# Pairing two 8x8 areas of one head in the score operands of a windowed attention kernel

## The chip, the cores and the metric

One NeuronCore of a Trainium2 chip runs the whole program. The metric is the device time of one execution in microseconds (us).

## The reference

The input x is (2, 128, 128, 128): batch, channels, rows, columns. Two residual blocks follow each other:

```
x = x + attention(gn(x));  x = x + conv3x3(gn(x)) + bias      gn: 32 groups of 4 channels
attention(x): g = clip((x*ac_w + ac_b)*x, 0, 6)
  qkv = qkv_w @ g                       16 heads of 8 channels; areas ("windows") of 8x8 = 64 pixels
  per area and head: o = softmax(q k^T / sqrt(8)) v
  out = proj_w @ o + proj_b
```

## The kernel before

Channels lie on the 128 partitions and the image of one batch stays in SBUF. For each batch the attention runs over 32 **units** of 8 areas (UT = 512 pixels); then the convolution runs over 16 strips of 8 rows. Its two phases are untouched by the change except for the memory that they lend.

The attention is a software pipeline. Every engine has its own list of steps per iteration i, written out by hand in a function `one`; `live(k)` says that unit i+k exists, and the step with n+k works k units ahead. The engines meet only at semaphores (`after` waits for the count of a unit). For one unit the steps are:

1. DVE makes aff, gpre and g32 (L667, L679, L703), ACT the high f16 part of g (L472), POOL the low part (L380).
2. PE projects keys and queries into the PSUM banks GB and GA (`project`, L853 to L855, three matmuls of 512 columns each) and the values in `v_rows` (L872, 12 matmuls of 128 columns).
3. ACT copies the high f16 part of q and k out of PSUM (L503, L495), DVE subtracts for the low part (L690, L692).
4. SP writes both to DRAM and reads them back in another layout. `write` (L261, L262) sends, per unit and operand, parts lo and hi (256 KB) and once more the high part (128 KB); `queries_in` (L272) reads 4 x 96 KB, `keys_in` (L280) 2 x 192 KB. On the score operands' 64 rows per row half r lie 48 rows of channel parts (two heads j, 8 channels, 3 parts) and two rows for the row maxima. Queries of head j stand in columns j, zeros elsewhere: `q_bd` holds [r, g, j, pixel].
5. `scores` (L885) does, for each of 4 pairs p of areas, 32 matmuls of 48 rows, 64 weights' columns and 64 moving columns, on the four quarters of the array (row half r, column half w). They fill the two banks S_B, of which there is one pair. DVE takes the row maxima from them (`row_max`, L654). PE turns the maxima of a unit (L975), ACT and DVE split them (L499, L686), and `maxima` (L288, 4 transfers of 8 KB) puts them into q_bd.
6. `scores_t` (L899) computes the scores again, transposed and with the maxima subtracted: 8 matmuls per pair of areas with 128 rows, 64 weights' columns and 256 moving columns, on two column halves. ACT takes the exponential (L448).
7. `weigh` (L918, L926) multiplies with the values and the ones, ACT and DVE make the quotient, POOL refines it (L370, L372), PE projects (L995), ACT and POOL add to the image (L476, L385), DVE collects statistics (L698).

The score operands have BUFS = 3 buffers, so the reads for unit d wait for the last `scores_t` of unit d-3 (`after(sp, st_done, d - BUFS)`). SP runs one list:

```
if live(3): queries_in(n + 3); keys_in(n + 3)
if live(2): maxima(n + 2)
if live(4): write(0, n + 4); write(1, n + 4)
```

SP's iteration i runs while PE is in its iteration i+1. PE projects unit n+3 in its iteration n and needs what was read in for n+2 before `scores(n + 2, 0)`, the third last score step of an iteration.

## Time and profile before

| what | value |
|---|---|
| three runs | 1206.22, 1206.10, 1197.05 us (median 1206.1) |
| profiled execution, whole time | 1207.08 us |
| its span | 1205.3 us, mean granted TensorE clock 0.947 |
| PE busy | 1015.8 us (84%) |
| weight loads (PEld) busy | 582.6 us (48%) |
| DVE busy | 983.1 us (82%) |
| ACT busy | 791.3 us (66%) |
| POOL busy | 503.8 us (42%) |
| L899 / L885 matmuls, busy | 163.8 us (x2048) / 118.6 us (x8192) |
| DMA | 140.59 MB, q1 share of 16 engines 36.3% |

Busy times of one engine count each instant once. PE and PEld overlap; "issue" is time in which the engine waited for nothing that the profile shows. Between the first and last L975 of a batch lie 31 units: from 67.1 to 443.9 us and from 663.1 to 1030.4 us.

### The profile page before, as it was taken

What the parts mean: (1) busy time and instruction counts of PE and PEld (TensorE: products, weight loads), DVE (VectorE), ACT (ScalarE), POOL (GpSimd) and SP (SyncE); (2) the same over time, 40 slices, a digit from 0 to 9 for tenths busy, and PEclk for the clock granted to TensorE, in tenths of its full rate; (3) what the DMA queues carried; (4) which work ended last, traced back from release to release, by engine and by line L of the source; (5) the groups of instructions that cost most, each with busy time, mean ns of one, the idle gap of its engine ahead of it and who ended that gap; (6) DMA issues with size and microseconds to landing.
All of it is one profiled execution on the core that took longest, in us unless ns stands there. A gap on an engine that the chain in (4) does not pass through costs nothing.

```text
span 1205.3 us, 52690 instructions
## 1 busy us (share of the span) xinstructions
PE 1015.8 (84%) x23011; PEld 582.6 (48%) x23011; DVE 983.1 (82%) x1312; ACT 791.3 (66%) x1327; POOL 503.8 (42%) x469
## 2 busy tenths in 40 slices
PE   0388999999999985998853899999999999779996
PEld 0155565556555652433321555556655655334442
DVE  6786888889888754899986788888988976379996
ACT  1257787778778774655532688878887877556663
POOL 5214454445444433233343245545454544404335
PEclk9879999999999997999986899999999999879998
DMA  8234444444444420133343454444444444001112
GB/s 307 84 118 125 136 138 138 136 137 128 135 142 135 142 64 1 44 129 108 105 157 122 123 150 139 136 137 138 144 132 148 134 142 126 4 1 53 70 70 88
DMA packets 114917, 140.59 MB, mean 117 GB/s; under 512 B 25088, under 2 KB 91008, under 8 KB 113664
## 3 DMA queue, kind: packets, MB, share of 16 engines
q1 hardware_dynamic: 114688, 137.23, 36.3%
q8 instruction: 182, 2.98, 1.1%
q14 instruction: 47, 0.39, 0.1%
HBM read 67.96 MB, written 67.11 MB: 112 GB/s over the span
## 4 chain that ended last, share of the span: by engine, by line
PE 63%; DVE 18%; issue 8%; DMA 4%; ACT 3%; SPq 2%; POOL 2%; POOLq 0%; DVEq 0%; ACTq 0%
PE ps L918 11%; PE ps L899 11%; PE ps L926 9%; PE ps L885 8%; PE ps L995 6%; PE ps L853 5%; DVE work L760 5%; PE ps L854 5%; PE ps L855 5%; DVE work L756 4%; PE ps L872 4%; DVE st L610 1%; SPq L288 1%; DVE work L738 1%; DMA q_bd<-stack_scratch 1%
## 5 line engine op out<-in xcount | busy, mean ns | idle before, releaser
L654 DVE TENSOR_REDUCE m_all<-ps 128x16 f32<-128x1024 f32 x256 | 313.5, 1225 | 114.9 <-PE ps L885 114.3
L370 POOL TENSOR_SCALAR work<-work 128x256 f32<-128x256 f32 x128 | 108.6, 849 | 401.2 <-DVE work L647 352.4
L885 PEld LDWEIGHTS ps<-k_pl,q_bd 48*64 48x64 f16 x8192 | 90.4, 111 | 174.5 <-issue 126.9
L448 ACT ACTIVATE late_probs<-ps,ws 128x1024 f32<-128x1024 f32 x128 | 142.8, 1116 | 44.6 <-PE ps L899 42.8
L853 PE MATMUL ps<-work,c_hi 128*128 128x512 f16 x384 | 148.3, 386 | 27.7 <-DVE work L760 27.7
L899 PE MATMUL ps<-q_bd,k_pl 128*64 128x256 f16 x2048 | 163.8, 282 | 7.5 <-ACT work L448 4.0
L885 PE MATMUL ps<-k_pl,q_bd 48*64 48x64 f16 x8192 | 118.6, 198 | 57.3 <-issue 39.4
L536 ACT CAST work<-work 128x512 f16<-128x512 f32 (+1 forms) x128 | 79.0, 622 | 115.8 <-DVE work L756 107.9
L448 ACT ACTIVATE work<-ps,ws 128x1024 f32<-128x1024 f32 x128 | 141.7, 1107 | 13.1 <-PE ps L899 11.5
L854 PE MATMUL ps<-work,c_lo 128*128 128x512 f16 x384 | 148.0, 385 | 0.0
L855 PE MATMUL ps<-work,c_hi 128*128 128x512 f16 x384 | 147.4, 384 | 0.0
L380 POOL TENSOR_TENSOR g_both<-work,g_both 128x512 f16<-128x512 f32 x64 | 99.9, 1561 | 54.4 <-ACT g_both L472 54.4
L899 PEld LDWEIGHTS ps<-q_bd,k_pl 128*64 128x64 f16 x2048 | 93.2, 110 | 58.7 <-issue 24.7
L647 DVE TENSOR_TENSOR work<-ps,work 128x512 f32<-128x512 f32 x128 | 87.3, 682 | 26.1 <-ACT work L457 26.1
L400 POOL TENSOR_TENSOR work<-work,img 128x512 f32<-128x512 f32 x30 | 48.1, 1603 | 139.3 <-DVE work L756 124.6
L760 DVE TENSOR_TENSOR work<-work 128x512 f16<-128x512 f32 (+1 forms) x128 | 101.7, 810 | 3.7 <-ACT work L536 3.1
L489 ACT COPY v_ext<-ps 64x256 f32<-64x256 f32 x256 | 93.3, 364 | 13.0 <-PE ps L872 8.1
L372 POOL TENSOR_TENSOR work<-work 128x256 f32<-128x256 f32 x128 | 93.2, 728 | 10.7
L455 ACT ACTIVATE work<-ps 128x256 f32<-128x256 f32 x128 | 49.2, 384 | 68.5 <-PE ps L926 68.5
L756 DVE TENSOR_TENSOR work<-g_both 128x512 f32<-128x512 f32 (+1 forms) x128 | 86.1, 693 | 4.8 <-ACT g_both L527 2.6
L918 PE MATMUL ps<-late_probs,v_ext 128*32 128x64 f32 x4096 | 87.6, 226 | 1.8 <-issue 1.6
L995 PE MATMUL ps<-work,pw 128*128 128x512 f32 x128 | 78.5, 698 | 7.0 <-POOL work L372 7.0
(126 smaller groups left out, 1894.1 us busy)
## 6 DMA issues: line engine op xcount, KB each, us to landing
stack_scratch<-work SPq DMA_DIRECT2D x128, 256.0 KB, 2.4
q_bd<-stack_scratch SPq DMA_DIRECT2D x256, 96.0 KB
k_pl<-stack_scratch SPq DMA_DIRECT2D x128, 192.0 KB, 3.5
stack_scratch<-work SPq DMA_DIRECT2D x128, 128.0 KB, 2.5
out_dram<-work SPq DMA_DIRECT2D x32, 512.0 KB, 2.9
img<-in_x_dram SPq DMA_DIRECT2D x8, 1024.0 KB, 13.4
img<-in_x_dram SPq DMA_DIRECT2D x16, 512.0 KB, 4.3
q_bd<-m_pair SPq DMA_DIRECT2D x256, 8.0 KB
```

Source lines behind the costliest of these rows:

```text
L370: g.tensor_scalar(near[h], near[h], -2.0, None, ALU.add).then_inc(less_done, 1)
L448: a.activation(probs[h][:, p % 2, :], ps[:, ST_B:ST_B + 2, :].rearrange("p w t -> p (w t)"), ACT.Exp, scale=ws[:, R_EXP:R_EXP + 1]).then_i ...
L654: v.tensor_reduce(m_all[:, 0, :, p], ps[:, S_B:S_B + 2, :].rearrange("p r (a k) -> p (r a) k", k=WIN), AX.X, ALU.max).then_inc(max_done, 1)
L756: v.tensor_tensor(plane[i][:, new_rows(t), :], column(t, l), column(t, r), op).then_inc(planes_done, 1)
L760: v.tensor_tensor(x_lo[:, i, ring_rows(t), :], plane[i][:, new_rows(t), :], x_hi[:, i, ring_rows(t), :], ALU.subtract).then_inc(x_lo_done, 1)
L853: t_.matmul(o, lhs_hi, rhs_hi, start=first, stop=False)
L854: t_.matmul(o, lhs_lo, rhs_hi, start=False, stop=False)
L855: return t_.matmul(o, lhs_hi, rhs_lo, start=False, stop=last)
L885: mm = t_.matmul(ps[64 * w:64 * w + 64, S_B + r, at:at + WIN], q_bd[rows, md, r, g, j, tok], k_pl[rows, md, g, tok], start=True, stop=True)
L899: mm = t_.matmul(ps[64 * c:64 * c + 64, ST_B + w, a * 256:a * 256 + 256], k_pl[:, md, g, tok], q_bd[:, md, :, g, :, tok], start=True, stop ...
L918: mm = t_.matmul(ps[32 * k:32 * k + 32, PV_B + h, at:at + WIN], v_ext[:, md, EACH * p + w, k, j:j + 2, :].rearrange("p s y -> p (s y)"), p ...
L995: t_.matmul(ps[:, GB, :], pw[:, :], o_n, start=True, stop=True).then_inc(proj_done, 1)
```

## The change

The score operands get another layout, and the queue of preparations gets one unit longer.

- On the 48 rows of a row half now lie 8 channels of **one** head, times two areas e of a pair (HE = 2), times 3 parts; the 8 heads of a half lie along g (HG = 8). A query of area 0 has zeros on the rows of area 1 and the other way round. These zeros are in the buffer `q_flat`, set by POOL once at the start and once ahead of batch 1 (the convolution's output buffer c_out[1] lies there), and they are sent along: the queries' writes and reads double (512 + 256 KB written, 2 x 384 KB read per unit). Keys hold 64 columns per pair: as many bytes as before, in rows of 512 bytes in place of 1 KB when read.
- `scores`: per pair of areas 16 matmuls of 48 rows, 128 weights' columns and 64 moving columns, on two row halves, in place of 32 on quarters.
- `scores_t`: per pair of areas 16 matmuls of 64 rows, 64 weights' columns and 128 moving columns on four quarters, in place of 8 on column halves.
- Projections of q and k, their splitting and their writes come 4 units ahead, not 3 (FIRST = 6); g gets four buffers. `queries_in` and `keys_in` of a unit now come one SP iteration after its writes (except for the first three units), behind the next unit's writes.
- The order of heads in probs, v and the output becomes the natural one, and proj_w is loaded by one transfer. SP issues 12 transfers per unit, not 14.

```
-HR, HG, HJ = 2, 4, 2
+HR, HG, HJ, HE = 2, 8, 2, 2
...
-ROWS = HJ * HD * PARTS
-HROWS = HD * PARTS
...
-FIRST = 5
+FIRST = 6
+G_BUFS = 4
...
-W_AT = -4
+W_AT = -5
...
-    stackd = nc.dram_tensor("stack_scratch", [BUFS, 2, P, PARTS, UT], F16, kind="Internal").ap()
+    q_stack = nc.dram_tensor("q_stack", [BUFS, P, HE, PARTS, UT], F16, kind="Internal").ap()
+    k_stack = nc.dram_tensor("k_stack", [BUFS, P, HE, PARTS, UT // HE], F16, kind="Internal").ap()
...
-        k_pl = sb("k_pl", [P, BUFS, HG, UT], F16)
-
-        q_bd = sb("q_bd", [P, BUFS, HR, HG, HJ, UT], F16)
+        k_pl = sb("k_pl", [P, BUFS, HG, UT // HE], F16)
+
+        q_bd = sb("q_bd", [P, BUFS, HG, UT], F16)
...
-        qk = part(1536, 1024).bitcast(F16).rearrange("p (s t) -> p s t", s=4)
+        k_parts = part(1536, 512).bitcast(F16).rearrange("p (e s x) -> p e s x", e=HE, s=2)
+        q_flat = part(7936, 1344).bitcast(F16)
+        g_parts = [(g_both[:, s * UT:s * UT + UT] if s < BUFS else part(2048, UT)).bitcast(F16).rearrange("p (k t) -> p k t", k=2)
+                   for s in range(G_BUFS)]
...
+        q_parts = q_flat[:, 0:2 * HE * UT].rearrange("p (e s t) -> p e s t", e=HE, s=2)
+
+        def queries(s):
+
+            both = q_flat[:, s * UT:s * UT + HE * (2 * UT + WIN)].rearrange("p (e y) -> p e y", e=HE)[:, :, 0:UT]
+            return both.rearrange("p e (a f t) -> p a e f t", a=PAIRS, f=HE)[:, :, :, 0, :]
+
+        def keys(s):
+
+            return k_parts[:, :, s, :].rearrange("p e (a t) -> p a e t", a=PAIRS)
+
+        def by_window(bank):
+
+            return ps[:, bank, :].rearrange("p (a e t) -> p a e t", a=PAIRS, e=HE)
...
-                def write(which, d, md, lo, sent):
-                    after(sp, lo, d)
-                    to = stackd[md, which]
-                    sp.dma_start(to[:, 0:2, :], qk[:, 2 * which:2 * which + 2, :]).then_inc(sent, 16)
-                    sp.dma_start(to[:, 2, :], qk[:, 1 + which, :]).then_inc(sent, 16)
+                def write_queries(d, md):
+                    after(sp, q_lo_done, d)
+                    sp.dma_start(q_stack[md, :, :, 0:2, :].rearrange("p e s t -> p e (s t)"),
+                                 q_parts.rearrange("p e s t -> p e (s t)")).then_inc(q_sent, 16)
+                    sp.dma_start(q_stack[md, :, :, 2, :], q_parts[:, :, 1, :]).then_inc(q_sent, 16)
+
+                def write_keys(d, md):
+                    after(sp, k_lo_done, d)
+                    sp.dma_start(k_stack[md, :, :, 0:2, :].rearrange("p e s x -> p e (s x)"),
+                                 k_parts.rearrange("p e s x -> p e (s x)")).then_inc(k_sent, 16)
+                    sp.dma_start(k_stack[md, :, :, 2, :], k_parts[:, :, 0, :]).then_inc(k_sent, 16)
 
                 def queries_in(d, md):
                     after(sp, q_sent, d)
                     after(sp, st_done, d - BUFS)
                     after(sp, q_in, d - 1)
-                    q_rows = stackd[md, 0].rearrange("(r g j d) s t -> r j (d s) g t", r=HR, g=HG, j=HJ)
+                    q_rows = q_stack[md].rearrange("(r g d) e s t -> r (d e s) g t", r=HR, g=HG)
                     for r in range(HR):
-                        for j in range(HJ):
-                            at = 64 * r + HROWS * j
-                            sp.dma_start(q_bd[at:at + HROWS, md, r, :, j, :], q_rows[r, j]).then_inc(q_in, 16)
+                        sp.dma_start(q_bd[64 * r:64 * r + ROWS, md, :, :], q_rows[r]).then_inc(q_in, 16)
 
                 def keys_in(d, md):
                     after(sp, k_sent, d)
                     after(sp, st_done, d - BUFS)
                     after(sp, k_in, d - 1)
-                    k_rows = stackd[md, 1].rearrange("(r g a) s t -> r (a s) g t", r=HR, g=HG)
+                    k_rows = k_stack[md].rearrange("(r g d) e s x -> r (d e s) g x", r=HR, g=HG)
                     for r in range(HR):
                         sp.dma_start(k_pl[64 * r:64 * r + ROWS, md, :, :], k_rows[r]).then_inc(k_in, 16)
 
...
                     for r in range(HR):
                         for k in range(2):
                             at = 64 * r + ROWS + k
-                            sp.dma_start(q_bd[at:at + 1, md, r, :, :, :].rearrange("o g j (a t) -> o (g j a) t", a=PAIRS),
+                            sp.dma_start(q_bd[at:at + 1, md, :, :].rearrange("o g (a t) -> o (g a) t", a=PAIRS),
                                          m_pair[32 * r:32 * r + 32, k, :]).then_inc(m_in, 16)
 
                 def one(i, m, live):
                     n = i + b * UNITS
-                    if live(3):
-                        queries_in(n + 3, (m + 3) % BUFS)
-                        keys_in(n + 3, (m + 3) % BUFS)
                     if live(2):
                         maxima(n + 2, (m + 2) % BUFS)
-                    if live(4):
-                        after(sp, q_in, n + 1)
-                        write(0, n + 4, (m + 4) % BUFS, q_lo_done, q_sent)
-                        after(sp, k_in, n + 1)
-                        write(1, n + 4, (m + 4) % BUFS, k_lo_done, k_sent)
+                    if live(5):
+                        after(sp, q_in, n + 2)
+                        write_queries(n + 5, (m + 5) % BUFS)
+                        after(sp, k_in, n + 2)
+                        write_keys(n + 5, (m + 5) % BUFS)
+                    if live(5) and i + 5 < BUFS:
+                        queries_in(n + 5, (m + 5) % BUFS)
+                        keys_in(n + 5, (m + 5) % BUFS)
+                    if live(4) and i + 4 >= BUFS:
+                        queries_in(n + 4, (m + 4) % BUFS)
+                        keys_in(n + 4, (m + 4) % BUFS)
...
+                    after(pool, out_done, b * CUNITS - 3)
+                    g.memset(q_flat[:, 0:2 * HE * UT].bitcast(F32), 0.0).then_inc(q_zero, 1)
...
+                    if live(4):
+                        to = g_parts[(i + 4) % G_BUFS]
+                        after(pool, g_hi_done, n + 4)
+                        g.tensor_tensor(to[:, 1, :], g32, to[:, 0, :], ALU.subtract).then_inc(g_lo_done, 1)
...
+                    if live(5):
+                        if b and i + 5 == BUFS:
+                            after(act, conv_done, b * CUNITS - 1)
+                        after(act, g32_done, n + 5)
+                        after(act, v_done, n + 5 - G_BUFS)
+                        a.copy(g_parts[(i + 5) % G_BUFS][:, 0, :], g32).then_inc(g_hi_done, 1)
...
-                        after(act, k_done, n + 3)
-                        after(act, k_sent, n + 2)
-                        a.copy(qk[:, 2, :], ps[:, GB, :]).then_inc(k_hi_done, 1)
+                    if live(4):
+                        after(act, k_done, n + 4)
+                        after(act, k_sent, n + 3)
+                        a.copy(keys(0), by_window(GB)).then_inc(k_hi_done, 1)
...
-                    if live(3):
-                        after(act, q_done, n + 3)
-                        after(act, q_sent, n + 2)
-                        a.copy(qk[:, 1, :], ps[:, GA, :]).then_inc(q_hi_done, 1)
+                    if live(4):
+                        if i + 4 == 0:
+                            act.wait_ge(q_zero, b + 1)
+                        after(act, q_done, n + 4)
+                        after(act, q_sent, n + 3)
+                        a.copy(queries(1), by_window(GA)).then_inc(q_hi_done, 1)
...
-                    if live(3):
-                        after(dve, q_hi_done, n + 3)
-                        v.tensor_tensor(qk[:, 0, :], ps[:, GA, :], qk[:, 1, :], ALU.subtract).then_inc(q_lo_done, 1)
-                        after(dve, k_hi_done, n + 3)
-                        v.tensor_tensor(qk[:, 3, :], ps[:, GB, :], qk[:, 2, :], ALU.subtract).then_inc(k_lo_done, 1)
+                    if live(4):
+                        after(dve, q_hi_done, n + 4)
+                        v.tensor_tensor(queries(0), by_window(GA), queries(1), ALU.subtract).then_inc(q_lo_done, 1)
+                        after(dve, k_hi_done, n + 4)
+                        v.tensor_tensor(keys(1), by_window(GB), keys(0), ALU.subtract).then_inc(k_lo_done, 1)
...
                     after(pe, max_done, d, p)
                     for g in range(HG):
-                        for j in range(HJ):
-                            for w in range(EACH):
-                                tok = slice((EACH * p + w) * WIN, (EACH * p + w + 1) * WIN)
-                                at = g * P + j * WIN
-                                for r in range(HR):
-                                    rows = slice(64 * r, 64 * r + ROWS)
-                                    mm = t_.matmul(ps[64 * w:64 * w + 64, S_B + r, at:at + WIN],
-                                                   q_bd[rows, md, r, g, j, tok], k_pl[rows, md, g, tok],
-                                                   start=True, stop=True)
+                        for r in range(HR):
+                            rows = slice(64 * r, 64 * r + ROWS)
+                            mm = t_.matmul(ps[:, S_B + r, g * WIN:g * WIN + WIN],
+                                           q_bd[rows, md, g, p * P:p * P + P], k_pl[rows, md, g, p * WIN:p * WIN + WIN],
+                                           start=True, stop=True)
                     mm.then_inc(s_done, 1)
...
-                    for w in range(EACH):
-                        tok = slice((EACH * p + w) * WIN, (EACH * p + w + 1) * WIN)
-                        for g in range(HG):
-                            a, c = g // 2, g % 2
-                            mm = t_.matmul(ps[64 * c:64 * c + 64, ST_B + w, a * 256:a * 256 + 256],
-                                           k_pl[:, md, g, tok], q_bd[:, md, :, g, :, tok],
+                    for g in range(HG):
+                        k, c = g // 2, g % 2
+                        for r in range(HR):
+                            rows = slice(64 * r, 64 * r + 64)
+                            mm = t_.matmul(ps[64 * c:64 * c + 64, ST_B + r, k * P:k * P + P],
+                                           k_pl[rows, md, g, p * WIN:p * WIN + WIN], q_bd[rows, md, g, p * P:p * P + P],
                                            start=True, stop=True)
                     mm.then_inc(st_done, 1)
...
                         else:
-                            after(pe, k_lo_done, n + 2)
-                        after(pe, g_lo_done, n + 3)
-                        project(1, GB, (m + 3) % BUFS, k_done)
+                            after(pe, k_lo_done, n + 3)
+                        after(pe, g_lo_done, n + 4)
+                        project(1, GB, (i + 4) % G_BUFS, k_done)
```

## Rows read from the trace of the kernel before

**Rows 1.** Fourth part of the page: the chain that ended last, by engine.

```profile
PE 63%; DVE 18%; issue 8%; DMA 4%; ACT 3%; SPq 2%; POOL 2%; POOLq 0%; DVEq 0%; ACTq 0%
```

**Rows 2.** Windows: us; PE, PEld, DVE, ACT, POOL busy; clock; DMA share; GB/s.

```profile
79.10:443.90 364.80, 341.22 (x10206) 213.48 (x10204) 299.98 (x375) 284.49 (x501) 170.87 (x175) 0.98 0.44 132
675.90:1030.40 354.50, 335.60 (x10205) 211.16 (x10204) 300.92 (x374) 283.80 (x500) 170.84 (x175) 1.00 0.46 136
...
350.30:361.50 11.20, 11.20 (x343) 7.02 (x341) 10.54 (x14) 9.67 (x19) 6.03 (x7) 1.00 0.40 126
```

**Rows 3.** Timeline of PE in that one unit: start us, us.

```profile
350.35 0.27 PE L975 MATMUL ps<-ident,m_all 128*128 128x128 f32 x1
...
352.55 0.45 PE L885 MATMUL ps<-k_pl,q_bd 48*64 48x64 f16 x32
...
356.95 0.63 PE L899 MATMUL ps<-q_bd,k_pl 128*64 128x256 f16 x8
357.51 0.45 PE L885 MATMUL ps<-k_pl,q_bd 48*64 48x64 f16 x32
357.88 0.29 PE L872 MATMUL ps<-w_hi,g_both 128*128 128x128 f16 x2
...
358.56 0.38 PE L853 MATMUL ps<-g_both,w_hi 128*128 128x512 f16 x1
```

**Rows 4.** Timeline of the weight loads (PEld) in that unit.

```profile
360.82 0.10 PEld L853 LDWEIGHTS ps<-g_both,w_hi 128*128 128x128 f16 x1
360.83 0.10 PEld L854 LDWEIGHTS ps<-g_both,w_lo 128*128 128x128 f16 x1
```

**Rows 5.** Timeline of DVE in that unit; in brackets idle before and its releaser.

```profile
349.82 1.18 DVE L679 SCALAR_TENSOR_TENSOR work<-img,cf,work 128x512 f32<-128x512 f32 x1
...
353.06 1.23 DVE L654 TENSOR_REDUCE m_all<-ps 128x16 f32<-128x1024 f32 x1 [0.28 <-PE ps L885]
...
360.95 1.18 DVE L679 SCALAR_TENSOR_TENSOR work<-img,cf,work 128x512 f32<-128x512 f32 x1
```

**Rows 6.** Chain of waits from 285 to 305 us, in order of time.

```profile
292.90 3.67 DMA stack_scratch<-work
...
299.09 3.77 DMA q_bd<-stack_scratch
...
304.06 0.45 PE ps L885 x32
```

**Rows 7.** Waits of the whole run: engine, line, awaited: us, times, longest.

```profile
PE ps L885 <- issue: 39.4, 34, 4.6
```

**Rows 8.** Timeline of SP's queue around one unit's transfers, and the PE rows near it.

```profile
313.98 2.42 SPq L288 DMA_DIRECT2D q_bd<-m_pair  x4
316.49 0.54 SPq L261 DMA_DIRECT2D stack_scratch<-work  x1
...
319.54 2.50 SPq L272 DMA_DIRECT2D q_bd<-stack_scratch  x4
322.15 0.79 SPq L280 DMA_DIRECT2D k_pl<-stack_scratch  x2
...
315.19 0.45 PE L885 MATMUL ps<-k_pl,q_bd 48*64 48x64 f16 x32
```

**Rows 9.** Windows with the DMA share and rate in the last two columns.

```profile
12.00:24.00 12.00, 1.59 (x6) 1.10 (x6) 11.05 (x29) 1.93 (x3) 9.22 (x1) 1.00 1.01 427
316.50:317.40 0.90, 0.90 (x22) 0.41 (x11) 0.90 (x2) 0.85 (x1) 0.00 (x0) 1.00 0.12 30
341.50:342.50 1.00, 1.00 (x28) 0.83 (x18) 1.00 (x3) 0.80 (x1) 0.00 (x0) 0.50 1.03 365
323.50:324.00 0.50, 0.50 (x33) 0.40 (x24) 0.50 (x1) 0.50 (x1) 0.42 (x2) 1.00 1.00 285
```

**Rows 10.** Timeline at the start of batch 0: SP, then PE.

```profile
49.31 0.33 SPq L261 DMA_DIRECT2D stack_scratch<-work  x1
57.71 0.53 PE L885 MATMUL ps<-k_pl,q_bd 48*64 48x64 f16 x22 [4.60 <-issue]
```

88 lines of the change are left out of this document (39 added, 49 removed).

## The prediction

> **What bounds the kernel now.** I read the chain of work that ended last first: TensorE (PE) holds 63% of it and "issue" 8%, DMA and SP together 6% [rows 1]. Then the time of one unit, from one turning of the maxima (L975, once per unit) to the next: 30 units of batch 0 took 364.8 us, 12.16 each, 30 of batch 1 354.5 us, 11.82 each [rows 2]. A unit in which PE never waits takes 360.95 - 349.82 = 11.13 us, read from one DVE step (L679) to the same of the next unit [rows 5]; there the reader is to see PE busy for all 11.20 us of the window, DVE for 10.54 and ACT for 9.67 [rows 2]. So PE sets the floor, DVE stands close behind it, and some 1.0 us (batch 0) or 0.7 us (batch 1) per unit is waiting.
>
> The waiting has one main place: the first score matmuls of a unit (L885), 39.4 us in 34 waits for something that is no engine's work [rows 7]. The chain shows what it is [rows 6]: the write to DRAM takes 3.67 us to land, the reads are issued only then, the last read of queries takes 3.77 us, and PE starts at 304.06, after the keys too. It is the loop split, write, read, score.
>
> **The change part by part.** I write S for the start of a unit's first L885.
>
> *Transposed scores.* A block of L899 takes 357.51 - 356.95 = 0.56 us for 8 matmuls of 256 columns, two side by side: 4 x 256 = 1024 column times, 0.43 us at 2.4 GHz (the clock is granted in full in this window), and 0.13 us of fill and switching. A block of L885 takes 357.88 - 357.51 = 0.37 us for 32 matmuls of 64 columns, four side by side: 8 x 64 = 512 column times, 0.21 us, and 0.16 us around them [rows 3]. The new L899 has 16 matmuls of 128 columns, four side by side: 4 x 128 = 512 column times, so 0.21 + 0.13 to 0.16 = 0.34 to 0.37 us. It saves 0.20 us per block, 4 blocks, **0.8 us of PE per unit**. That all four quarters run together with 64 rows is what L885 shows with 48.
>
> *Scores.* 16 matmuls of 64 columns, two side by side, are 8 x 64 = 512 column times again: half the instructions, the same 0.37 us. What could differ is the loading of 128 weights' columns next to only 64 moving ones. The bounds: L872 has a 128-column load for each of 12 matmuls in 358.56 - 357.88 = 0.68 us, 57 ns each, so a load takes at most that [rows 3]; as two row halves load side by side this gives 8 x 57 + 160 = 0.61 us, +0.24 per block and +1.0 us per unit. The other end is two loads that start 0.01 us apart on the same array (360.82 and 360.83) [rows 4]: the path of a load is free again after about that long, 16 of them fit into 0.21 us, and nothing is added. I take nothing, for these are the only rows in which a load isn't held back by long matmuls. A gain below nothing is excluded by the column times.
> The Trainium skill ("TensorE: Matmul & The Clock Gate", LDWEIGHTS) gives a load as its columns divided by 1.2 per ns, 107 ns for 128 columns. By that a score block would take 8 x 107 + 160 = 1.0 us, and a unit of PE 2.6 us more. The 57 ns per load of L872 [rows 3] already speak against it.
>
> So PE's floor falls from 11.13 to 10.3 us, and DVE's counts: the 11.13 us between two L679 hold 0.28 us of idle time for scores in between and two more such waits of 0.19 and 0.17 us [rows 5]: 10.5 us of DVE per unit. Its work and ACT's stay the same in kind and size (512 elements per split; the strided targets keep runs of 64 elements). **Engine floor: 10.5 us**, held by DVE.
>
> *Bytes.* Per unit before: 768 KB written, 768 KB read. After: queries 768 + 768 KB, keys 384 + 384 KB, 2304 KB. Rates with all DMA engines busy: 365 GB/s for this write, 285 GB/s for reads in 1 KB rows, 427 GB/s for the input in 8 KB rows [rows 9]. Over 16 engines a row of 8 KB takes 307 ns and one of 1 KB 57 ns, hence about 21 ns per row and 36 ns per KB, and 39 ns for 512 bytes. Queries: 786 KB/365 = 2.2 us written, 786/285 = 2.8 read. Keys: 1.4 us written (256 rows of 57 ns and 256 of 39 over 16), 768 x 39/16 = 1.9 read. **Sum 8.3 us of all DMA engines per unit**, against 5.4 now (0.44 of 12.16 [rows 2]). Bounds: at 365 GB/s for all, 6.5 us; at the reads' rate for all and 57 ns for each of the 1024 rows of 512 bytes, 2359/285 + 1024 x 28.5/16 = 10.1 us.
>
> *The loop with the longer lead.* Now: S is 315.19; SP issues maxima until 316.40, writes from 316.49, reads from 319.54 to 322.94 [rows 8]; data flow about 0.9 us after an issue (DMA share 0.12 up to 317.40 [rows 9]). The wait for the landing of the write before each read goes: reads of unit n+4 are issued behind the writes of n+5 and wait only for the last transposed scores of n+1, ready at about S + 1. SP's queue is: four maxima to S + 1.2, four writes (2.4 us now) to S + 3.7, four reads (two issues fewer, 0.4 each by L280's 0.79 for two) to S + 5.3. The data begin at S + 2.2, and 8.3 us of work end at S + 10.5; with landing S + 11.0. What is late next is this: reads are due at the next S, 10.5 us later by the engines. If PE waits x there, the maxima and the splitting of the unit were done x earlier relative to S, and the writes too; the period is P = 10.5 + x and P = 11.0 - x, so **P = 10.75 us**. Behind SP's waits stand the next maxima, needed only at the following L899; it comes 356.95 - 352.55 = 4.4 us after S [rows 3], 4.2 with the shorter block between, and they are issued by S + 1.2: 3 us are left for their landing behind what remains of the reads.
> To this comes unevenness (late landings, slow issues such as L272's 2.50 us for four), which costs 1.0 and 0.7 us per unit now; the same loop, with less reserve but without the landing wait, keeps about half: 0.45 us. P = 11.2 us. With 6.5 us of transfers in place of 8.3 it is 10.8 (A below), with 10.1 it is (10.5 + 12.8)/2 + 0.45 = 12.1.
>
> *Fill and drain.* At each batch's start the write of unit 0 is issued at 49.31 and its scores start at 57.71 [rows 10]. Writes and reads of unit 0 grow by half, 1.2 + 1.6 us at the rates above, and q and k of a third unit must be split ahead of DVE's first maximum: 2.5 us later per batch, 5 in all. POOL's extra memset ahead of batch 1, the waits for c_out and for the convolution's last matmuls lie beside work that takes longer (POOL is busy for 503.8 us in all); uncovered they would be about 1 us once. The shorter last units are in the average below.
>
> **The sum**, against the profiled execution of 1207.1 us: batch 0 31 x (12.16 - 11.2) = 29.8 us, batch 1 31 x (11.82 - 11.2) = 19.2 us, less 5: 44 us. 1207 - 44 = **1163 us**; the profiled execution lies 1 us above the median of 1206.1.
>
> **Rivals.**
> A. *The transfers hide and DVE alone sets the pace.* If mixed writes and reads run at 365 GB/s, 6.5 us, the loop has 1.3 us in hand and P is 10.5 + 0.3. 31 x (1.36 + 1.02) - 5 = 69 us: 1138. For it speaks 365 GB/s in writes; against it that 1 KB reads never pass 285 [rows 9]. The Trainium skill ("DMA: Bandwidth & Descriptors", Specifications) says that rows of 512 bytes and more run at line rate, which would favour A; no row before shows it.
> B. *Weights of 128 columns don't hide.* PE's floor is 10.3 + 1.0 = 11.3 us, over DVE's and the transfers': P = 11.55 with small unevenness, 31 x (0.61 + 0.27) - 5 = 22 us: 1185. For it: the load of 128 columns has never run next to 64. Against it rows 4.
> C. *DMA throughput takes over: slower.* Place: the reads before L885. Reads now go out right behind the writes, and no row shows both at full load; if they cost each other 30% of the 285 GB/s, 2.36 MB take 11.8 us. From about 11.4 us of transfers on, P is over 12.0 and all gain is gone. At 11.8, P = 11.8 + 0.3 for the maxima + 0.45 = 12.55: 31 x (0.39 + 0.73) + 5 = 40 us slower: 1247. For it: the DMA share rises from 0.45 to about 0.75 and any fetch of instructions then delays one of 16 engines. Against it: 285 GB/s is the lowest rate at full load here.
> D. *The stall isn't the transfers' latency but moves along* (P near 11.9 as the lead brings nothing and the bytes take what PE gives): 1207, no change.
>
> **Chances.** Forecast (P from 10.95 to 11.45: 1148 to 1179) 0.48; A 0.17; B 0.11; C 0.12; D 0.12. The range for 8 in 10 is 1130 to 1210: it leaves out most of C and the end of A. A difference of 1%, 12 us, is about what a measurement of this kernel can tell from none. Faster by over 1% (forecast, A, most of B): 0.74; within it: 0.12; slower: 0.14.
>
> **What would show it.** L899's blocks at 0.35 us and L885's at 0.37; 0.6 would be B. A unit without waits of 10.5 to 10.8 us, DVE busy in over 95% of it. DMA share near 0.75 and some 210 GB/s in the attention's windows. The waits of L885 on "issue" still there but shorter; gone would be A, longer and in every unit C. The sum would be wrong if L899's quarters didn't run together, if a split into strided f16 took longer than the 0.6 to 0.7 us of now, or if maxima came late behind the reads and L899 waited at the head of a unit.

## The result and the profile after

The changed kernel took 1357.5 us (median of four runs, 1344.8 to 1367.7) against 1204.4 us for the kernel before (1197.1 to 1206.2): a ratio of 1.125, 95% interval 1.115 to 1.135. The ratio leaves out the slowest run, which is over 1.5% above the fastest. The kernel is slower by an eighth, where 1163 us were forecast. Its profiled execution has a span of 1359.1 us at a mean granted clock of 0.89.

The page of the changed kernel: engines, DMA queue, the chain that ended last by engine, the two reads. They answer to [rows 1] and to the table of before.

```profile
PE 1022.6 (75%) x20963; PEld 577.2 (42%) x20963; DVE 975.3 (72%) x1312; ACT 788.3 (58%) x1327; POOL 499.5 (37%) x471
...
q1 hardware_dynamic: 193648, 187.55, 57.7%
...
PE 30%; DMA 24%; DVE 15%; issue 13%; SPq 8%; ACT 8%; POOL 1%; POOLq 0%; ACTq 0%; DVEq 0%
```

PE's share of the chain has fallen from 63% to 30%, DMA's has risen from 4% to 24%. The busy time of the engines is about what it was (PE's 0.8 us per unit that the new blocks save are hidden by a lower clock: with half the queries' bytes, in half_both below, PE is busy for 970.9 us); what has been added is waiting.

Windows of the changed kernel: the 31 units of each batch, then two neighbouring units, then a stretch of writes, one behind a long wait of PE, and one of reads. They answer to [rows 2] and [rows 9].

```profile
76.10:512.40 436.30, 346.68 (x9386) 213.98 (x9386) 302.39 (x380) 286.98 (x507) 170.08 (x175) 0.89 0.74 165
740.50:1185.40 444.90, 347.15 (x9385) 214.71 (x9386) 301.70 (x380) 286.67 (x507) 170.17 (x175) 0.90 0.74 162
965.10:983.70 18.60, 12.93 (x310) 7.96 (x309) 10.16 (x14) 9.46 (x18) 5.99 (x7) 0.82 0.93 190
983.70:994.40 10.70, 10.33 (x311) 6.42 (x309) 10.21 (x14) 9.57 (x18) 5.89 (x7) 1.00 0.40 126
990.00:993.00 3.00, 2.84 (x82) 1.92 (x79) 3.00 (x5) 2.67 (x6) 0.90 (x2) 1.00 1.00 348
973.00:976.00 3.00, 3.00 (x66) 2.04 (x61) 2.51 (x4) 1.44 (x2) 0.00 (x0) 0.50 0.76 234
996.00:999.00 3.00, 0.57 (x12) 0.09 (x4) 1.29 (x2) 1.85 (x4) 1.54 (x2) 1.00 1.18 164
```

A unit took 436.3/31 = 14.07 us in batch 0 and 444.9/31 = 14.35 us in batch 1, against 12.15 and 11.85. The average hides two kinds of unit that often take turns, as here: 18.6 us, and 10.7 us right behind it. The row from 990 and the last one are the first clue: with all DMA engines busy the writes move 348 GB/s, the reads 164.

PE's timeline over the two units, whose start is the turning of the maxima (L1000), answers to [rows 3].

```profile
965.05 0.27 PE L1000 MATMUL ps<-ident,m_all 128*128 128x128 f32 x1
...
972.84 0.61 PE L913 MATMUL ps<-k_pl,q_bd 48*128 48x64 f16 x16 [5.61 <-issue]
...
979.60 0.42 PE L927 MATMUL ps<-q_bd,k_pl 64*64 64x128 f16 x16
979.95 0.41 PE L913 MATMUL ps<-k_pl,q_bd 48*128 48x64 f16 x16
980.29 0.28 PE L904 MATMUL ps<-w_hi,g_both 128*128 128x128 f16 x2
...
983.73 0.27 PE L1000 MATMUL ps<-ident,m_all 128*128 128x128 f32 x1
...
986.01 0.41 PE L913 MATMUL ps<-k_pl,q_bd 48*128 48x64 f16 x16
...
990.12 0.42 PE L927 MATMUL ps<-q_bd,k_pl 64*64 64x128 f16 x16
```

A scores_t block (L927) now takes 979.95 - 979.60 = 0.35 us and a block of scores (L913) 980.29 - 979.95 = 0.34 us. The first L913 of the long unit waited 5.61 us. Behind that wait the granted clock is at its lower level, 0.50 or 1.2 GHz (window from 973): the same steps from the first L913 to the last L927 of the iteration took 979.60 - 972.84 = 6.76 us there and 990.12 - 986.01 = 4.11 us in the next unit, 2.65 us more.

The chain of waits of the changed kernel, in order of time, answers to [rows 6]; SP's queue in the second unit to [rows 8].

```profile
963.76 6.43 DMA q_bd<-q_stack
970.20 2.65 issue
972.84 0.61 PE ps L913 x16
...
989.39 3.27 DMA q_stack<-work
992.66 0.30 SPq L291
...
993.00 7.03 DMA q_bd<-q_stack
1000.03 1.68 issue
1001.71 0.61 PE ps L913 x16
```

```profile
985.13 3.54 SPq L307 DMA_DIRECT2D q_bd<-m_pair  x4
988.78 0.57 SPq L275 DMA_DIRECT2D q_stack<-work  x1
989.39 0.62 SPq L277 DMA_DIRECT2D q_stack<-work  x1
990.11 1.42 SPq L281 DMA_DIRECT2D k_stack<-work  x1
991.57 0.63 SPq L283 DMA_DIRECT2D k_stack<-work  x1
992.31 1.20 SPq L291 DMA_DIRECT2D q_bd<-q_stack  x2
993.62 0.92 SPq L299 DMA_DIRECT2D k_pl<-k_stack  x2
```

The wait is for the reads: the queries' last lands at 1000.03, the keys', issued behind it, at 1001.62, and PE starts at 1001.71 (the chain puts the stretch behind the queries' landing down to "issue"). A read of 384 KB takes 6.5 us to land; one of before took 3.77 us for the last of four [rows 6]. Two theories stood at this point: the reads are slow (by their bytes, by rows of 512 bytes, or by where they go), or something of the rest is (the lead, the doubled writes, the 128 columns, the new order of PE). The expectations below say in place what each theory holds; their numbers were given as the theories came up, so the text here names them by content.

### The profile page after: what moved, and what is told of

Its sections match the earlier page's. It is cut to its first block, busy times and chain, and to the rows that moved or that the text cites. A ratio compares the mean times of both kernels' runs of the same rounds, so it can differ in the third digit from the quotient of the medians.

```text
span 1359.1 us, 48466 instructions
## 1 busy us (share of the span) xinstructions
PE 1022.6 (75%) x20963; PEld 577.2 (42%) x20963; DVE 975.3 (72%) x1312; ACT 788.3 (58%) x1327; POOL 499.5 (37%) x471
## 4 chain that ended last, share of the span: by engine, by line
PE 30%; DMA 24%; DVE 15%; issue 13%; SPq 8%; ACT 8%; POOL 1%; POOLq 0%; ACTq 0%; DVEq 0%
DMA q_bd<-q_stack 14%; DMA q_stack<-work 7%; PE ps L947 6%; SPq L307 5%; PE ps L1020 5%; DVE work L792 4%; PE ps L954 4%; DVE work L788 3%; ACT work L476 3%; PE ps L913 3%; PE ps L885 3%; PE ps L886 3%; PE ps L887 3%; PE ps L927 3%; ACT v_ext L519 2%
## 5 line engine op out<-in xcount | busy, mean ns | idle before, releaser
L913 PE MATMUL ps<-k_pl,q_bd 48*128 48x64 f16 x4096 | 114.5, 200 | 141.8 <-issue 111.5
L913 PEld LDWEIGHTS ps<-k_pl,q_bd 48*128 48x128 f16 x4096 | 82.9, 100 | 266.9 <-issue 175.6
L927 PE MATMUL ps<-q_bd,k_pl 64*64 64x128 f16 x4096 | 115.9, 233 | 29.8 <-issue 10.2
L947 PE MATMUL ps<-work,v_ext 128*32 128x64 f32 x4096 | 92.1, 230 | 24.6 <-issue 24.6
L927 PEld LDWEIGHTS ps<-q_bd,k_pl 64*64 64x64 f16 x4096 | 70.8, 112 | 86.3 <-issue 36.3
L1020 PE MATMUL ps<-work,pw 128*128 128x512 f32 x128 | 94.0, 824 | 7.0 <-POOL work L399 7.0
L947 PE MATMUL ps<-late_probs,v_ext 128*32 128x64 f32 x4096 | 98.9, 246 | 0.5 <-issue 0.3
L408 POOL TENSOR_TENSOR g_both<-work,g_both 128x512 f16<-128x512 f32 x48 | 74.8, 1558 | 64.2 <-ACT g_both L502 64.2
L399 POOL TENSOR_TENSOR work<-work 128x256 f32<-128x256 f32 x128 | 93.2, 728 | 10.7
```

What stands on the lines that cost most here:

```text
L913: mm = t_.matmul(ps[:, S_B + r, g * WIN:g * WIN + WIN], q_bd[rows, md, g, p * P:p * P + P], k_pl[rows, md, g, p * WIN:p * WIN + WIN], star ...
L927: mm = t_.matmul(ps[64 * c:64 * c + 64, ST_B + r, k * P:k * P + P], k_pl[rows, md, g, p * WIN:p * WIN + WIN], q_bd[rows, md, g, p * P:p * ...
L947: mm = t_.matmul(ps[32 * k:32 * k + 32, PV_B + h, at:at + WIN], v_ext[:, md, EACH * p + w, k, j:j + 2, :].rearrange("p s y -> p (s y)"), p ...
L1020: t_.matmul(ps[:, GB, :], pw[:, :], o_n, start=True, stop=True).then_inc(proj_done, 1)
```

## The experiments

**transfers**: the transfers alone, each kind four times, issued and awaited, nothing else running; it computes nothing.

```
q_after  = 2 reads x (48 partitions x 8 KB), rows of 1 KB        kernel line 70
quarters = the same in 4, lower and upper half in turn           72
k_after  = 2 x (48 x 4 KB), rows of 512 bytes; k_before: 1 KB    75, 77
q_before = 4 x (24 partitions x 4 KB)                            79
one half alone (48), 96, 128 partitions at once                  82, 84, 86
```

> This kernel computes nothing; it makes the transfers of both kernels by themselves, each pattern four times with a wait for the landing between (and the first input copied to the output). Theory 1 (a read into 48 neighbouring partitions is held back by the place that it writes to in SBUF, and by rows of 512 bytes not costing less than rows of 1 KB): 768 KB of queries into 2 x 48 partitions take 4 us or more of data flow after the first byte (under 200 GB/s), the same bytes into 128 partitions (s_j) flow at 280 GB/s or more, one half alone (s_h, 384 KB) takes more than half as long as both, and alternating the two halves in four transfers (s_d) is faster than s_c by 15% or more; the keys in 512-byte rows (s_e, 384 KB) take as long as 768 KB in 1 KB rows would by row count. Theory 2 (reads alone are as fast as I assumed, 285 GB/s whatever the partitions, and only the mixture of writes and reads is slow): s_c takes 2.8 us of data flow, s_d the same, and s_e 1.9.

SP's timeline of this kernel, the four repetitions of a kind merged into a row; a repetition takes the distance to the next row's start, divided by four.

```profile
31.87 20.64 SPq L70 DMA_DIRECT2D q_new<-q_stack  x8
58.41 19.46 SPq L72 DMA_DIRECT2D q_new<-q_stack  x16
82.21 12.44 SPq L75 DMA_DIRECT2D k_new<-k_stack  x8
97.59 12.33 SPq L77 DMA_DIRECT2D k_old<-o_stack  x8
112.89 12.84 SPq L79 DMA_DIRECT2D q_old<-o_stack  x16
127.84 12.61 SPq L82 DMA_DIRECT2D q_one<-q_stack  x4
144.40 16.26 SPq L84 DMA_DIRECT2D q_wide<-q_stack  x4
165.64 12.98 SPq L86 DMA_DIRECT2D q_full<-q_stack  x4
182.52 0.53 SPq L59 DMA_DIRECT2D q_stack<-src  x1
```

The new reads of queries take (58.41 - 31.87)/4 = 6.6 us, in four smaller transfers in turn 5.95, 96 partitions at once 5.3, all 128 partitions (182.52 - 165.64)/4 = 4.2 us, and half the bytes into one half of the partitions 4.1 us. Keys in rows of 512 bytes take 3.85 us, in rows of 1 KB 3.8: the short rows cost nothing. The Trainium skill ("DMA: Bandwidth & Descriptors", Specifications) says that 512 bytes suffice for line rate; these rows agree. Two expectations were missed here: turns bring 10%, not 15%, and the short rows were to cost something.

Some 0.95 us pass from the first issue to the first packet. Windows from the first to the last packet of one repetition, for q_after, 96 and 128 partitions:

```profile
32.84:37.67 4.83, 0.00 (x0) 0.00 (x0) 1.00 1.00 163
145.38:148.97 3.59, 0.00 (x0) 0.00 (x0) 1.00 0.89 219
166.61:169.49 2.88, 0.00 (x0) 0.00 (x0) 1.00 0.70 273
```

So the data flow at 163 GB/s into the halves one behind the other and at 273 into all 128 partitions. The expectations for wide_reads below have 2.2 us for the latter, which takes 2 us of latency off the 4.2; the packets show 2.9. Nor is this row a test of the destination alone: its packets are rows of 6 KB in DRAM, those of all other reads of queries 1 KB. The row of 96 partitions, 64 of one half and 32 of the other, has rows of 1 KB and points the same way. The Trainium skill ("SBUF — State Buffer", Door 1: The DMA Port Swizzle) has partitions 0 to 63 on 8 of the 16 ports and 64 to 127 on the other 8; a slower rate into one half is in accord with that. That the destination holds a read back rests on full_width and full_halves below, whose rows and bytes are the same.

**lead_only**: the kernel before with q, k and their writes 4 units ahead, layout and bytes as before. **quarters_only**: the kernel before with transposed scores in quarters. **both**: lead and quarters together, no pairing, no zeros sent.

```
+FIRST = 6; G_BUFS = 4                          # lead_only, both
+if live(5): write(0, n + 5 ...); write(1, n + 5 ...)
+if live(4): queries_in(n + 4 ...); keys_in(n + 4 ...)
...
-k_pl[:, md, g, tok], q_bd[:, md, :, g, :, tok]           # quarters_only, both
+k_pl[rows, md, g, tok], q_bd[rows, md, r, g, :, tok]     # for r in range(HR)
```

> The kernel before with the longer lead alone (projections, splitting and writes of q and k 4 units ahead, reads one iteration of SP's list after their writes; old layout, old matmuls, old bytes). Theory 1 (the doubled queries made the transfers longer than a unit; the lead itself is sound): the waits of the first score block mostly go, a unit takes 11.2 to 11.5 us, about 1175 us in all. Theory 3 (the new order of SP's list is what hurts: reads queue behind the next unit's writes): no gain or slower, 1205 to 1260 us.

> The kernel before with the transposed scores alone in quarters: 16 matmuls of 64 rows and 128 moving columns per pair of areas, each row half into its own bank (probs and what reads them follow); old stacks, old transfers, old lead. The block should take 0.35 us, PE's floor fall to 10.3 us and DVE hold 10.5; the waits for the transfers stay or grow, as they close the loop in 10.5 to 11 us: about 11.4 us per unit, 1170 us in all. If the transfers' loop is as long as the unit already, nothing is gained: 1200.

> The kernel before with the longer lead and the transposed scores in quarters, but the old stacks and their bytes: all of the change except the pairing of areas with its zeros. Theory 1: a unit takes 10.7 to 11.0 us, the engines' floor, 1135 to 1145 us in all. Theory 3: 1200 or more.

lead_only took 1181.3 us, ratio 0.989 (0.983 to 0.995), 11.45 and 11.60 us per unit, 27 of 57 units within 0.15 us of PE's floor of 11.14 us. PE's waits for "issue" at the first score block fall from 39.4 us to 12.6. The lead itself gains, though less than was expected (1175 us, a ratio of 0.974 to the 1206 of then). quarters_only took 1216.6, ratio 1.018 (1.012 to 1.025), and both 1196.5, ratio 1.001 (0.998 to 1.005). Both were expected to be much faster: PE is busy for 968.9 and 970.6 us, against 1015.8 before. PE's timeline shows where that went, here of both, then of the changed kernel.

```profile
312.36 0.34 PE L909 MATMUL ps<-q_bd,k_pl 64*64 64x128 f16 x11
313.15 0.27 PE L909 MATMUL ps<-q_bd,k_pl 64*64 64x128 f16 x5 [0.46 <-issue]
...
1168.96 0.43 PE L947 MATMUL ps<-work,v_ext 128*32 128x64 f32 x16
1173.54 0.66 PE L947 MATMUL ps<-work,v_ext 128*32 128x64 f32 x16 [4.14 <-issue]
```

A block breaks off after 11 of 16 matmuls, or 16 of 32, and goes on later, with no wait in the program between. I count such a break where two neighbouring PE instructions of one line start over 0.6 us apart and the second waits for no semaphore; the output projection (L995 before) is left out, whose one matmul shows as two records 0.53 us apart.

| kernel | breaks | us in all | PE records |
|---|---|---|---|
| before | 3 | 3 | 46022 |
| lead_only | 8 | 7 | 46022 |
| quarters_only | 54 | 51 | 50118 |
| both | 61 | 57 | 50118 |
| both_light | 62 | 54 | 50118 |
| both_fewer | 15 | 14 | 41926 |
| half_both | 12 | 11 | 41926 |
| half_reads | 19 | 16 | 41926 |
| interleave | 11 | 11 | 41926 |
| changed kernel | 23 | 44 | 41926 |
| reads_first | 44 | 117 | 41926 |

(PE records are its matmuls and weight loads; the kernels further down are explained there.) The DMA packets in the traces tell what the breaks go with. Every page has a queue "q8 instruction", of packets of 16 KB, and PE has 253 records per packet in every kernel (46022 to 182 packets, 50118 to 198, 41926 to 166). Of the 471 breaks in the 19 kernels that run the attention, 469 end 1.15 to 1.8 us after the end of such a packet; of all PE instructions in the attention 10 to 17% start in that stretch. The reading is that PE stood without instructions there; no run that follows hastens or delays these packets by itself.

**half_reads**: the changed kernel reads queries only for 4 of the 8 groups g. **half_writes**: from the fourth unit on it writes queries only for area 0 of each pair. **half_both**: both. The operands left out hold old data.

```
-q_bd[64 * r:64 * r + ROWS, md, :, :], q_rows[r]
+q_bd[64 * r:64 * r + ROWS, md, 0:HG // 2, :], q_rows[r][:, 0:HG // 2, :]     # half_reads
...
+es = slice(0, HE) if d < BUFS else slice(0, 1)    # half_writes: q_stack[md, :, es, ...]
```

> The changed kernel, but only heads 0 to 3 of the 8 along g of each row half are read into q_bd (the queries of the other heads stay zero, so their scores are left out of the result): 384 KB less to read per unit, the same matmuls and waits. Theory 1 (the loop of write, read and score is what a unit waits for, and reads into 48 partitions run at some 170 GB/s): the reads get 2.3 us shorter, the stall of every second unit falls from about 5 us to about 1, its cold clock with it: 11.5 to 12.1 us per unit, 1190 to 1230 us in all. Theory 4 (the new forms of the matmuls or the new order of SP's list cost the time): at most 2% better than 1357.

> The changed kernel, but after the first three units only the rows of area 0 of the queries are written to DRAM (those of area 1 stay those of an early unit, so half the scores are of old queries): 384 KB less to write per unit, reads unchanged. By the loop, writes stand ahead of the reads in the queues: 1.1 us shorter, P from (10.5 + 13.3)/2 down by 0.5 and less cold clock: 12.8 to 13.5 us per unit, 1270 to 1315 us. If only the reads' place counts (they wait for nothing but their own flow), nothing: 1350.

> Both omissions together, so that the bytes per unit are those of before, with the changed layout's matmuls, lead and waits. If bytes alone explain the change's loss, it lands where the same kernel without the pairing of areas landed (1196 us), 1185 to 1215. If the 128-column weights or the layout cost time of their own, above 1230.

half_reads took 1219.4 us, ratio 1.008 (1.004 to 1.012); half_writes 1352.2, ratio 1.119 (1.112 to 1.126); half_both 1192.8, ratio 0.986 (0.979 to 0.993). 384 KB less of reads per unit take away 138 of the 153 us lost, 384 KB less of writes 5. The latter was expected to bring 42 us or more, and the miss tells how the loop is built: in the median unit of half_writes the writes have landed 9.8 us after L1000 in place of 11.2, but from the first read's issue to the last landing 9.4 us pass in place of 9.5. Most of the writes' data flow before those of the reads begin. And half_both, which has the paired layout without the doubled bytes, needs nothing more for its weights of 128 columns: by the ratios it is 1.6% faster than both (1.001), which has more PE instructions and 57 us of breaks in place of 11.

**interleave**: the changed kernel, queries read by four transfers, lower and upper half of the partitions in turn.

```
+for k in range(2):  gs = slice(HG // 2 * k, HG // 2 * k + HG // 2)
+    for r in range(HR):  q_bd[64 * r:64 * r + ROWS, md, gs, :], q_rows[r][:, gs, :]
```

> The changed kernel with the queries' reads issued as four transfers that alternate between the two row halves (g 0 to 3 of half 0, of half 1, then g 4 to 7), same bytes and rows. By themselves such reads took 5.95 us from issue to issue in place of 6.5. Theory 1: 0.5 us off the loop, 0.3 to 0.6 us per unit with the clock, 1320 to 1340 us. If the place in SBUF doesn't matter beside the writes: 1357, or slower by SP's two more issues.

It took 1309.4 us, ratio 1.085 (1.076 to 1.094): 48 us faster than the changed kernel with the same bytes and two issues more, and better than expected. The reading is that two 384 KB transfers issued one behind the other keep to one half of the partitions for most of their time and smaller ones in turn overlap better; from the first read's issue to the last landing 9.1 us pass in place of 9.5, and the breaks fall from 44 to 11 us.

**both_fewer**: both, without the values of every second head (128 PE instructions fewer per unit). **both_light**: both, reading one of four groups g for queries and keys. **lead_swap**: lead_only with its four query reads in turn for the lower and the upper half.

```
-for j in range(HJ):                  # weigh
+for j in range(1):                   # both_fewer
...
-q_bd[at:at + HROWS, md, r, :, j, :], q_rows[r, j]
+q_bd[at:at + HROWS, md, r, 0:1, j, :], q_rows[r, j][:, 0:1, :]     # both_light; keys too
...
-for r in range(HR): for j in range(HJ):
+for j in range(HJ): for r in range(HR):                            # lead_swap
```

> The kernel with the longer lead and the transposed scores in quarters, but the values of every second head are left out when the weights are applied: 128 fewer of PE's instructions per unit, the transfers as before; so the output differs from the reference. DVE's 10.5 us per unit stand as before. Theory 5 (the blocks of many short matmuls are interrupted because PE's instructions, which come over the same DMA engines, don't arrive in time): fewer instructions come with less waiting, the gaps inside blocks fall from 102 us to about 50 us or less, the time from 1196 to 1150 to 1170 us. Rival (the gaps have nothing to do with the number of instructions, or the pace is set by the loop of transfers): PE only stands still longer before its first score block, 1185 to 1196 us.

> The kernel with the longer lead and the quarters, but only one in four groups of heads is read back for queries and keys; the others' operands are left as they were, so the output differs from the reference. Writes, waits and all instructions of PE stay. Theory 5: with the DMA engines less loaded the instructions arrive in time, the gaps inside blocks fall from 102 us to below 60 us; as the wait for the reads ends too, the time goes to the engines' floor: 10.5 to 10.8 us per unit, about 1150 to 1165 us. Rival (the instruction supply is bound by itself, whatever the DMA engines do): gaps stay near 100 us and the time at 1180 us or more.

> The kernel before with the longer lead alone, and the four reads of queries issued in turn for the lower and the upper half of the partitions, not two of one half first. If transfers into one half of the partitions hold each other back, the reads land some 0.5 us earlier: 1170 to 1180 us against 1181. If only the landing wait counted, which the lead has removed: 1181, the same.

both_fewer took 1166.7 us, ratio 0.968 (0.963 to 0.973), with 14 us of breaks in place of 57: with fewer instructions they mostly go, as expected. Their number alone isn't the cause: lead_only has more instructions than both_fewer and fewer breaks. both_light took 1183.8, ratio 0.983 (0.979 to 0.988), with 54 us of breaks: in this kernel they do not come from the reads' load on the DMA engines, and that half of the theory falls. By the ratios it was still 1.8% faster than both; its reads land 2.1 us ahead of the first score block in the median unit in place of 0.7. lead_swap took 1187.8, ratio 0.987 (0.983 to 0.991), no different from lead_only: with four transfers of 24 partitions the order of halves brings nothing.

**wide_reads**: the changed kernel, queries in DRAM padded by 16 rows of zeros behind every 48, read by one transfer of 1 MB into 128 partitions. **padded_halves**: the same, read by two of 512 KB.

```
+q_stack = nc.dram_tensor("q_stack", [BUFS, HG, HR, 64, UT], ...)
+for r in range(HR): two writes from partitions 64 * r to 64 * r + 63
+q_bd[:, md, :, :], q_stack[md].rearrange("g r x t -> (r x) g t")             # wide_reads
+q_bd[64 * k:64 * k + 64, md, :, :], q_stack[md, :, k].rearrange("g x t -> x g t")   # padded_halves
```

> The changed kernel with its queries in DRAM padded by 16 rows of zeros per 48, so that one transfer of 1 MB fills all 128 partitions of the operand, in place of two of 384 KB that fill 48 each; the bytes read grow by a third, from 1152 to 1408 KB per unit with the keys. Theory 2 (a read into one half of the partitions is held back by its destination: 4.6 us of data for the two, and 2.2 us for 768 KB over all 128 partitions, measured alone): the queries' data take about 3 us, 1.6 us less per unit of the loop; half of it is seen in the period, and the cold clock behind the long stalls goes partly too: 1280 to 1315 us. Rival (the bytes read are the cost, wherever they go): a third more bytes of queries, 1.5 us more in the loop, 1390 to 1410 us.

> As wide_reads, the same DRAM layout, the same bytes and writes, but read by two transfers of 512 KB, one for each half of the partitions. Theory 2: a third more to push into each half, about 6.1 us of data in place of 4.6: 1390 to 1420 us. Rival (bytes alone): the same as wide_reads.

1442.9 us, ratio 1.199 (1.190 to 1.208), and 1474.5, ratio 1.224 (1.216 to 1.233). Each is outside the range of either theory. SP's timeline of wide_reads shows that the experiment changed something else.

```profile
398.17 0.64 SPq L284 DMA_DIRECT2D q_stack<-work  x1
...
404.51 0.73 SPq L300 DMA_DIRECT2D q_bd<-q_stack  x1
```

The writes had to be split by halves, and SP spent 10.9 us per unit on issues in place of 8.6; the read goes out 6.3 us after the first write, not 3.5. The pair of runs still differs by 32 us with the same bytes, in the direction of the destination. padded_halves has one issue more, though.

**full_width** and **full_halves** repair that. Heads are ordered g first and r second on q's and k's partitions, each channel has 8 rows in DRAM (6 as before, 2 for the constants and the maxima), and so reads can fill 128 partitions from writes that stay as they are.

```
+q_stack = nc.dram_tensor("q_stack", [BUFS, P, 8, UT], ...); k_stack: [BUFS, P, 8, UT // HE]
+rows = q_stack[md].rearrange("(g h) y t -> (h y) g t", g=HG)
+for at, many in READS: q_bd[at:at + many, md, :, :], rows[at:at + many]
+READS = ((0, 128),)              # full_width
+READS = ((0, 64), (64, 64))      # full_halves
```

> The changed kernel with another order on the 128 partitions: the heads' pairs come first and the row half second, every channel has 8 rows in DRAM (6 as before and 2 that hold the operands' constants, written once), so that one transfer of 1 MB fills all 128 partitions with queries and one of 512 KB with keys, in place of 2 x 384 and 2 x 192 KB into 48 partitions each. Writes are the same transfers from 128 partitions with the same bytes, unlike those of wide_reads, which were issued per half; SP issues 10 transfers per unit in place of 12; scores take 64 rows in place of 48. Theory 2 (a read is held back by the half of the partitions that it goes to): 1.5 MB at the 340 GB/s of the queries' reads in wide_reads are 4.6 us, against some 7 us for 1.15 MB in the changed kernel; the loop is 2.4 us shorter, half of it or somewhat more comes off the period, the long stalls and the cold clock behind them go: 1200 to 1260 us. Rival (bytes are the cost): 1390 us or more.

> As full_width, same rows, bytes and writes, but queries and keys are each read by two transfers, one for each half of the partitions. Theory 2: 1.5 MB into halves at 170 GB/s are over 9 us, 2 us more than in the changed kernel: 1400 to 1450 us. Rival: within 20 us of full_width.

full_width took 1301.3 us, ratio 1.079 (1.075 to 1.083), full_halves 1378.0, ratio 1.144 (1.140 to 1.149). With the same bytes and writes the destination makes 77 us, and full_width is 56 us faster than the changed kernel although it reads a third more. That bytes are the cost whatever the destination would have been two equal times above 1390. In the median unit 8.6 us pass from the first read's issue to the last landing in full_width, 10.3 in full_halves, 9.5 in the changed kernel; breaks make 18, 48 and 44 us. full_halves also issues two transfers more; interleave, which issues two more than the changed kernel and is faster, speaks against that as the cause. But full_width missed its own range by 40 us, and full_halves was better than its own. Windows in which reads are under way, full_width first:

```profile
347.00:353.00 6.00, 6.00 (x179) 3.93 (x179) 4.93 (x6) 4.51 (x9) 2.79 (x4) 1.00 0.97 284
```

```profile
363.00:369.00 6.00, 4.56 (x134) 2.61 (x132) 4.89 (x7) 5.53 (x12) 4.38 (x4) 1.00 1.08 226
```

284 against 226 GB/s. At 284 GB/s 1.5 MB still need 5.5 us.

**reads_first, full_first, lead_first**: the changed kernel, full_width and lead_only, each with the reads of unit n+4 moved ahead of the writes of n+5 in SP's list.

```
 maxima(n + 2, ...)
+if live(4) and i + 4 >= BUFS: queries_in(n + 4 ...); keys_in(n + 4 ...)
 if live(5): after(sp, q_in, n + 2); write_queries(n + 5 ...); ...
-if live(4) and i + 4 >= BUFS: queries_in(n + 4 ...); keys_in(n + 4 ...)
```

> The changed kernel with one block of SP's list moved: the reads of unit n+4 (whose writes were issued an iteration ago) stand ahead of the writes of n+5 and not behind them. In the changed kernel the first read is issued 7.7 us after the turning of the maxima and the next unit's scores are due at 12.8; here it is issued at 4.1. Theory 6 (the loop counts SP's queue ahead of the reads and then the reads' data, which don't get slower or faster by the order): 3.5 us earlier, so of the stalls of 4 to 5 us in every second unit about 1 is left, and the clock stays warm: 1180 to 1240 us. Rival a (the DMA engines' throughput is used up, whatever the order): 1330 us or more. Rival b (the reads then wait for the last transposed scores of unit n+1 and the queue stands still in front of the writes): 1280 to 1330 us.

> full_width with the same block of reads ahead of the writes. Theory 6 with theory 2: reads issued at 4.1 us, 1.5 MB at 284 GB/s in 5.5 us, landed at about 10.5 of the 12.8 us that they have: no stalls are left, the engines' floor of 10.5 us and the unevenness of 0.3 to 0.6 us count, 1150 to 1180 us, and faster than the kernel with the longer lead alone (1181). If writes behind the reads hold up the splitting of the next unit: 1190 to 1220.

> The kernel before with the longer lead, reads ahead of the writes. Its first block of scores still waits in about half of the units. Theory 6: those waits end, PE's own floor of 11.13 us remains, 1165 to 1175 us; rival b: 1181 or more.

1496.1 us, ratio 1.244 (1.239 to 1.250); 1422.7, ratio 1.184 (1.180 to 1.188); 1268.3, ratio 1.055 (1.052 to 1.059). All three are clearly slower. For reads_first that is what the rival of a used-up throughput gave in numbers, and yet not for its reason; full_first is outside all its ranges, and lead_first got what its rival said, and more. The waits of reads_first (engine, line, awaited: us, times, longest):

```profile
DVE m_pair L718 <- ACT m_pair L529: 288.1, 64, 7.4
ACT work L525 <- DMA k_stack<-work: 277.0, 60, 7.1
```

L525 is ACT's copy of the next unit's keys; it may overwrite the one buffer only when the last write has landed. Behind the reads the writes land 7.7 us after their issue in the median, ACT stands, and the splitting of the maxima that follows on ACT (L529), for which DVE waits, stands behind it. lead_first shows the same pair with 117.3 and 107.7 us. In reads_first the breaks of PE's blocks grow to 117 us as well; what of the loss is theirs isn't separated. The theory that only the reads' place in the queue counts falls: the transfers of a unit have two due times, the writes before the next split and the reads before the next scores, and moving one ahead breaks the other.

The fastest kernel that computes everything is the kernel before with the longer lead alone: lead_only at 0.989 (0.983 to 0.995) and lead_swap at 0.987 (0.983 to 0.991), which are one result.

## Why the prediction was wrong

**Right.** *What bounded the kernel before*, and the place of its waits: lead_only changes nothing but the lead, its waits there fall by two thirds, and it gains 1.1%. *The transposed scores*: 0.35 us per block, forecast 0.34 to 0.37. *The 128 columns*: 16 weights are loaded in a block of 0.34 us. The Trainium skill ("TensorE: Matmul & The Clock Gate", LDWEIGHTS) gives a load of 128 columns 107 ns. The rows agree, at 100 ns for the mean load of L913, but the loads overlap, and the 1.0 us for a block that the prediction worked out from that figure did not come. *The engine floor*: 10.5 us was the sum, and the unit without a wait shows 10.66 us between L1000 at 983.73 and the next at 994.39, with DVE busy in 95%. *The mechanism*: a loop through SP's queue and the transfers that ends at the first block of scores, period (10.5 + C)/2.

**The step that failed** is the last sum of "The loop with the longer lead": with "8.3 us of work" and the data beginning at S + 2.2 it had C = 11.0. Measured in the unit of 983.7: S is 986.01, the writes' data begin at 990, that is S + 4.0, and the next unit's scores start at 1001.71, that is S + 15.7. In the median of 54 units the first read goes out 7.8 us after L1000 and the last lands at 17.4; S is 2.3 us after L1000 in a unit without a wait. So C is 15.1: 5.5 us of SP's queue in place of 3.7, and 9.6 us from the first read's issue to the last landing in place of 7.3. In order of size:

1. *The size of the transfers' term.* "786/285 = 2.8" us for the queries' reads took 285 GB/s from half a microsecond [rows 9]. The two windows behind it in the kernel before, of the same reads, show that it was a peak and not a rate:

```profile
324.00:324.50 0.50, 0.50 (x3) 0.24 (x2) 0.50 (x2) 0.50 (x2) 0.50 (x1) 1.00 1.09 207
324.50:325.00 0.50, 0.50 (x8) 0.26 (x8) 0.50 (x1) 0.50 (x3) 0.50 (x2) 1.00 0.88 160
```

The changed kernel's two transfers fill one half of the partitions each, one behind the other: 164 GB/s at full load, 163 and 4.8 us when run alone. Transfers took 0.74 of 14.2, 10.5 us of all DMA engines per unit, in place of 8.3, and above the upper bound of 10.1. half_reads, interleave and full_width against full_halves show this term. Of the 8.3 us, the writes' 3.6 (3.7, as the keys' 1.4 should be 1.5) hardly belong in C at all: by the sum half_writes should have gained 34 us and it gained 5.
2. *SP's queue.* Maxima and four writes were put down with 3.7 us from S to the first read; the maxima's issues end 4.1 us after L1000, the writes' 7.65. From the first write's issue to the first read's it is 3.5 us, forecast 2.4. That is 1.6 to 1.8 us more of C; lead_only has its first read at 6.5 us in place of 7.8 by the same measure. No run changed this term by itself.
3. *The clock.* The prediction had no term for what a long wait leaves behind: the clock at half, 2.65 us in the unit that follows the wait.
4. *PE's instructions.* It had no term for the breaks either: 44 us in the changed kernel, 3 before. They fall to 16 with half the queries read and to 11 with the reads in turn. How much of them is hidden in waits isn't known.
5. *Fill and drain.* "2.5 us later per batch, 5 in all": the first L1000 comes at 76.1 us in place of 67.1, and from the last of batch 0 to the first of batch 1 it is 228.1 us in place of 219.2, 18 us in all.

With C = 15.1 the prediction's own formula gives (10.5 + 15.1)/2 = 12.8 us, and 2.65 us in every second unit make 14.1; measured are 14.07 and 14.35. That this comes so near is in part luck, for unevenness and breaks are not in it.

**The rivals.** The time went beyond C, the slower one (1247). Its place was right, the reads before L913, and so was its condition, throughput of the reads; its reason, writes and reads that disturb each other at full load, is not what the runs show: half_writes gains next to nothing. Its point of decision, 11.4 us of transfers, was too high already by the prediction's own formula, (10.5 + C)/2 + 0.45, which passes 12.0 us at C = 12.6, that is 9.9 us of transfers. "285 GB/s is the lowest rate at full load here", said against it, was wrong by the rows above. B, the weights' loading, is refuted by the blocks of 0.34 us and by half_both.

**What would have been missed even with the right rate.** both and half_both, which have the lead, the short scores and the old bytes, reach ratios of 1.001 and 0.986. By the prediction's sum 10.5 us per unit and its 0.45 of unevenness would be 1207 - 31 x (1.21 + 0.87) = 1143 us, a ratio of 0.95. "It saves 0.8 us of PE per unit" is right as PE's busy time and brings no time: blocks of more and shorter matmuls break off, 57 us in all in both against 7 in lead_only, and each break ends shortly behind a packet of PE's instructions. Why about one packet in three brings a break in both and one in 23 in lead_only, and why the breaks get longer where reads are long, stays open; no run changed how instructions arrive.

**Also open**: why an issue of SP takes 0.4 us at one time and 1.7 at another, and how much of full_width's remaining loss (ratio 1.079 against 0.986 for half_both) belongs to its 0.67 of 13.3, 8.9 us of transfers, and how much to the queue. A second buffer for q's and k's parts, which would let reads go ahead of writes, was not tried.
